# Last stage of a two-layer model: the norm's closing steps, the finish of the last block, and who forms the remainders of the running sums

## The chip, the cores and the metric

One core of one Trainium2 chip. The metric is the device time of one execution in microseconds (us). The kernel before took 3646.28 us (median of 3 runs, 3641.34 to 3650.77). All times below are us unless ns is written.

## The reference, cut to what matters

Two layers, one after the other, on x of shape (2, 2048, 512). The first is an attention layer with a feed-forward part and is not touched. The second is the last stage of the kernel, called `average` in the code:

```python
def _L1_cond_ref(inputs, vector, attention_weights, temperature, values, operator, ff1, ff1_bias, ff2, ff2_bias, ln_gamma, ln_beta):
    att = ...                                        # one gate per token and head
    v = jnp.einsum('bsi,ihk->bshk', inputs, values)
    cumv = jnp.cumsum(v, axis=1)                     # running sum over the tokens
    attn_out = att[..., None] * cumv / denom[..., None]
    op = attn_out.reshape(...) @ operator + vector[:, None, :]
    res = jax.nn.relu(jnp.concatenate([inputs, op], -1) @ ff1 + ff1_bias)
    res = res @ ff2 + ff2_bias + inputs
    mu = jnp.mean(res, axis=-1, keepdims=True)
    var = jnp.mean(jnp.square(res - mu), axis=-1, keepdims=True)
    xhat = (res - mu) * jax.lax.rsqrt(var + EPS_LN)
    return xhat * ln_gamma + ln_beta
```

## The kernel before, in words

`program` runs four stages; `average` (from L1450) is the last. It works on NA = 8 blocks of 512 tokens. Every matmul operand is held as two rounded parts, a high one (names in h: `ch`, `ah`, `sh`, `xh`) and the remainder, a low one (`cl`, `al`, `sl`, `xl`), and each product is three passes: high by high, high by the weight's low part, low by high. The running sum over tokens is taken on the input (a scan on VectorE, `running_sum`, L1760) and multiplied by the values weights afterwards.

Each engine has a program of its own, and semaphores order them. TensorE's order (the loop that follows `rows_out`) is written out by hand. For block n it is:

1. `values(n, 0)`: 12 matmuls (L1626). The first four wait for `c_hi` (the four high parts of the block's running sums, ScalarE's `sum_hi`, L1690), the last four for `c_lo` (their remainders, GpSimd's `sum_lo`, L1857).
2. `open_relu(n)`: 48 matmuls (L1609), the input's share of the hidden layer, into four PSUM accumulators.
3. `rows_out(n-1, j)` for the four tiles j of 128 tokens of the block before: 48 matmuls (L1655), the product with ff2.
4. For h = 1 to 7: `values(n, h)` and `gated(n, h-1)` (L1641), 12 matmuls each; then `gated(n, 7)`.

VectorE multiplies each `values` result by its gate (`av_full`, L1834), ScalarE rounds it (`av_gated_hi`, L1735), GpSimd forms the remainder (`av_gated_lo`, L1875); `gated(n, h)` needs both. Between these, VectorE does the norm of the block before: adds the residual rows (L1769) and takes the statistics (L1773 to L1780) at h = 0, and at h = 1 to 4 one tile each of `normed`: (row - mean) * rstd (L1789), then times gamma (L1794). GpSimd adds beta (`shifted`, L1852) and SyncE stores the tile (L1554). At h = 4 to 7 VectorE also does, for one quarter each of the next block, `zT_lo` (L1745, after ScalarE's `zT_hi`, L1680) and `running_sum` (L1760 and a small copy, L1762), and GpSimd adds the bias b2 to one tile (`zb`, L1886).

After `gated(n, 7)` ScalarE takes the hidden layer out of PSUM: `relu` (L1700) into `av_full` and a rounding copy (L1705) for each of four accumulators, from the third on only when GpSimd has formed the remainder (L1870) of the one two before, since `av_full` has two buffers. GpSimd's program has its four `sum_lo` ahead of these remainders.

The last block has nothing beside it: `relu`, the remainders, `rows_out` for four tiles, and then on VectorE two halves of two tiles each (`HALVES`), with the normalising of the first half placed after the statistics of the second.

## Time and profile before

| | |
|---|---|
| median of 3 runs (range) | 3646.28 (3641.34 to 3650.77) |
| the profiled execution: its time | 3638.28 |
| its span, first to last instruction | 3636.5 |
| mean granted TensorE clock, share of 2.4 GHz | 0.976 |
| the stage `average`, within the span | from about 3009 to 3636.5 |
| busy in the span: TensorE, VectorE, ScalarE, GpSimd | 95%, 56%, 42%, 57% |

The profile comes from one profiled execution; every time in its rows is us from the start of the span. "Busy" is the time in which an engine had an instruction under way. The matmuls are pipelined: a group of twelve takes 2.80 from the start of its first to the start of the next group, though each is listed with about 0.4. In a row of the timeline the last bracket is the idle time ahead of the instruction and what ended it.

### The profile page before, as it was taken

To read this page: it belongs to the slowest core of one execution; us is meant where nothing else is said; L and a number is where in the kernel's file an instruction comes from. 1 tells how busy PE (TensorE), PEld (TensorE's weight loads), DVE (VectorE), ACT (ScalarE), POOL (GpSimd) and SP (SyncE) were. 2 spreads that over 40 slices of the span, in tenths; PEclk is the share of its full clock that TensorE was granted. 3 is DMA by queue.
4 is the path that set the end of the run, shared out by engine and by line. 5 is a ranking of instruction groups with operands and counts; after the bars stand their busy time and mean duration, and the time that the engine had idled before them with its cause. 6 is when DMAs were issued, how large, how long until landed. Compare 5 with 4: busy or idle time off the path is not lost. (4 is left out here: it accounts for less than half of the span.)

```text
span 3636.5 us, 47173 instructions
## 1 busy us (share of the span) xinstructions
PE 3445.7 (95%) x16672; PEld 2249.6 (62%) x16672; DVE 2049.4 (56%) x3299; ACT 1513.1 (42%) x2791; POOL 2090.9 (57%) x1663
## 2 busy tenths in 40 slices
PE   7999899999999999999999969999999986999997
PEld 6777445454554545455455348888888864777776
DVE  5776677777777777777777244222222213434433
ACT  2332366666666666666666632111111112211121
POOL 3654388888988888788888712222222213544553
PEclk9999899999999999999999979999999997999999
DMA  4555676868778786967765453212222114222220
GB/s 171 183 173 197 119 146 125 157 132 152 145 129 151 135 148 125 151 140 133 152 124 111 102 150 97 70 59 76 73 70 69 57 38 145 82 73 70 74 75 37
DMA packets 176739, 419.34 MB, mean 115 GB/s; under 512 B 15382, under 2 KB 62998, under 8 KB 151670
## 3 DMA queue, kind: packets, MB, share of 16 engines
q1 hardware_dynamic: 153606, 249.59, 26.1%
q0 software_dynamic: 22896, 166.73, 23.8%
q8 instruction: 132, 2.16, 0.3%
q14 instruction: 105, 0.86, 0.1%
HBM read 162.25 MB, written 87.03 MB: 69 GB/s over the span
## 5 line engine op out<-in xcount | busy, mean ns | idle before, releaser
L845 DVE TENSOR_REDUCE part_max<-ps_att 128x1 f32<-128x512 f32 x1972 | 1226.6, 683 | 391.7 <-PE ps_att L763 390.9
L891 ACT ACTIVATE probs<-ps_att 128x512 f32<-128x512 f32 x2048 | 1062.1, 602 | 537.4 <-PE ps_att L735 456.8
L942 POOL TENSOR_TENSOR prob_sums<-prob_sums,probs 128x512 f32<-128x512 f32 x884 | 1145.8, 1558 | 56.4 <-DMA probs<-probs 56.3
L787 PE MATMUL ps_att<-probs,v_tok 128*32 128x512 f32 x4096 | 548.1, 607 | 0.0
L1433 POOL TENSOR_TENSOR ff_g_lo<-ff_g,ff_g_hi 128x512 fp32r<-128x512 f32 x128 | 165.1, 1290 | 552.4 <-DVE ff_g_hi L1394 552.4
L735 PE MATMUL ps_att<-q_stack,k_first 97*128 97x512 f32 x768 | 326.7, 425 | 10.3 <-ACT probs L891 10.0
L735 PE MATMUL ps_att<-q_stack,k_stack 97*128 97x512 f32 x768 | 321.3, 426 | 11.1 <-ACT probs L891 10.5
L1302 ACT ACTIVATE ff_g<-ps_ff 128x512 f32<-128x512 f32 x128 | 76.7, 599 | 579.7 <-PE ps_ff L1186 579.7
L763 PE MATMUL ps_att<-k_first,q_stack 96*128 96x512 f32 x756 | 302.4, 400 | 7.2 <-DMA q_stack<-qk 7.2
L763 PE MATMUL ps_att<-k_stack,q_stack 96*128 96x512 f32 x768 | 303.7, 395 | 0.0
L735 PEld LDWEIGHTS ps_att<-q_stack,k_stack 97*128 97x128 f32 x768 | 143.8, 189 | 199.2 <-ACT probs L891 146.8
L735 PEld LDWEIGHTS ps_att<-q_stack,k_first 97*128 97x128 f32 x768 | 145.9, 190 | 194.2 <-ACT probs L891 138.3
L1875 POOL TENSOR_TENSOR av_gated_lo<-av_full,av_gated_hi 128x512 fp32r<-128x512 f32 x64 | 92.5, 1445 | 282.3 <-ACT av_gated_hi L1735 282.3
L924 POOL DMA_DIRECT2D probs<-probs x159 | 151.6, 954 | 177.2 <-PE ps_att L787 160.9
L1394 DVE CAST ff_g_hi<-ff_g 128x512 fp32r<-128x512 f32 x128 | 54.8, 428 | 299.4 <-ACT ff_g L1302 299.4
L787 PEld LDWEIGHTS ps_att<-probs,v_tok 128*32 128x32 f32 x4096 | 80.8, 108 | 183.3 <-ACT probs L891 171.6
L942 POOL TENSOR_TENSOR prob_sums<-probs 128x512 f32<-128x512 f32 x128 | 164.8, 1422 | 48.7 <-DMA probs<-probs 46.1
L553 POOL TENSOR_TENSOR rotated<-rot_a,rot_b 128x512 f32<-128x512 f32 x64 | 89.8, 1403 | 153.2 <-DVE rot_b L394 149.5
L763 PEld LDWEIGHTS ps_att<-k_first,q_stack 96*128 96x128 f32 x756 | 145.2, 192 | 34.1 <-DMA q_stack<-qk 7.8
L763 PEld LDWEIGHTS ps_att<-k_stack,q_stack 96*128 96x128 f32 x768 | 145.6, 190 | 26.3
L1834 DVE TENSOR_TENSOR av_full<-ps_avg,av_gate_rows 128x512 f32<-128x512 f32 x64 | 44.3, 692 | 191.5 <-PE ps_avg L1626 84.1
L1735 ACT ACTIVATE av_gated_hi<-av_full 128x512 fp32r<-128x512 f32 x64 | 40.5, 633 | 258.7 <-DVE av_full L1834 258.7
(202 smaller groups left out, 5795.7 us busy)
## 6 DMA issues: line engine op xcount, KB each, us to landing
probs<-probs POOLq DMA_DIRECT2D x159, 1024.0 KB, 8.6
q_stack<-qk SPq DMA_DIRECT2D x144, 128.0 KB, 7.2
qk<-rot_hi SPq DMA_DIRECT2D x64, 256.0 KB, 6.6
qk<-rot_lo SPq DMA_DIRECT2D x64, 256.0 KB, 2.5
av_gate_rows<-gate SPq DMA_DIRECT2D x64, 256.0 KB
k_stack<-qk SPq DMA_DIRECT2D x24, 512.0 KB, 11.0
k_first<-qk SPq DMA_DIRECT2D x18, 512.0 KB, 10.9
x_in_sb<-in_x SPq DMA_DIRECT2D x8, 1024.0 KB, 6.7
```

The source lines that it names most:

```text
L553: nc.gpsimd.tensor_tensor(rot[:, u % 2, :], ra[:, u % 2, :], rb[:, u % 2, :], ALU.add)\
L735: nc.tensor.matmul(sT[u % 3], kS[b][0:S3 + 1, h, k * P:(k + 1) * P], q_rows(n)[0:S3 + 1, h, :], start=True, stop=True)\
L763: nc.tensor.matmul(mx[mx_uses % 3], q_rows(n)[0:S3, h, q * P:(q + 1) * P], kS[b][0:S3, h, k * TB:(k + 1) * TB], start=True, stop=True).the ...
L787: mm = nc.tensor.matmul(o_ps[rows, :], t["v"][:, steps[w]["b"], k, rows], t["p"][:, w % PR, h, :], start=(k == 0), stop=(k == LT - 1))
L845: nc.vector.tensor_reduce(t["pm"][:, r, k:k + 1], mx[mx_uses % 3], AX.X, ALU.max)\
L891: nc.scalar.activation(t["p"][:, at % PR, h, :], sT[(at * G + h) % 3], ACT.Exp)\
L924: nc.gpsimd.dma_start(t["p"][:, w % PR], t["p"][:, (w + 1) % PR], accum_op=ALU.add).then_inc(sem, 16)
L942: nc.gpsimd.tensor_tensor(x, first, t["p"][:, w % PR, h, :], ALU.add).then_inc(s["acc_done"], 1)
L1302: nc.scalar.activation(gf[:], ps[:, 4 + u % 2, :], ACT.Gelu_apprx_tanh).then_inc(s["g"], 1)
L1394: nc.vector.tensor_copy(gh[:, u % 2, :], gf[:]).then_inc(s["g_hi"], 1)
L1433: nc.gpsimd.tensor_tensor(gl[:, u % 2, :], gf[:], gh[:, u % 2, :].bitcast(F32), ALU.subtract)\
L1875: nc.gpsimd.tensor_tensor(al[:, v % 2, :], af[:, v % 2, :], ah[:, v % 2, :].bitcast(F32), ALU.subtract).then_inc(s["a_lo"], 1)
```

## The change

- The norm's closing steps become two operations with two tensors and a scalar each (scalar_tensor_tensor), both on VectorE: `centred`, (row - mean) * gamma, and `normed`, row * rstd + beta. GpSimd's `shifted` and the semaphore `ga` are gone; the store waits for `normed`.
- `zT_hi`, `zT_lo` and `running_sum` of the next block run at h = 3 to 6 instead of 4 to 7. `sum_hi` of the first quarter stands at h = 7 ahead of that h's rounding copy; the other three stay behind it.
- `sum_lo` of quarters 0 and 1 goes to VectorE, behind h = 7, for every block but the first; quarters 2 and 3 stay on GpSimd.
- Last block: ScalarE writes the rounded hidden layer straight out of PSUM (`last_relu`); VectorE recomputes it unrounded and forms the remainders (`last_relu_lo`). TensorE starts on the first accumulator that is ready, and runs the two passes on high parts of tiles 0 and 1 before their third passes (`last_rows_out`). VectorE takes the four tiles one by one through all steps.

```diff
--- before.py
+++ after.py
@@ -1491,13 +1491,12 @@
             uses += [("af", n, h) for h in range(1, HC)] if n < NA else []
         at_use = {u: i for i, u in enumerate(uses)}
         per_block = {"t": TT, "af": HC}
-        HALVES = (slice(0, 2), slice(2, TT))
         parts = ((a["ff1"], fh, fl, slice(0, 4)), (a["values"], vh, vl, slice(0, 2)), (a["values"], vh, vl, slice(2, 4)),
                  (a["wp"], wh, wl, slice(0, 4)), (a["wp"], wh, wl, slice(4, 8)), (a["ff2"], eh, el, slice(0, 4)))
         weights = [[x[:, at, :].rearrange("p k n -> p (k n)") for x in (src, hi, lo)] for src, hi, lo, at in parts]
         stage = [x.rearrange("p j f -> p (j f)") for x in (z[:, 0], z[:, 1], zTr[:, 1])]
         FF1, VAL, WP, FF2 = 0, 2, 3, 5
-        LOW_POOL = 3
+        LOW_POOL, PARTS_AT, SUMS_DVE = 3, HC - DC - 1, (0, 1)
 
         def bank(*use):
             return ring[at_use[use] % 4]
@@ -1642,19 +1641,33 @@
                                                   stop=(h == HC - 1 and i == 2))
                     mm.then_inc(s["aw"], 1)
 
-                def rows_out(n, j):
-                    pe.wait_ge(s["r_hi"], DC * (n + 1))
-                    wait_bank(pe, "t", n, j)
+                def rows_out(n, j, passes=range(3)):
+                    if 0 in passes:
+                        wait_bank(pe, "t", n, j)
                     if n == 0 and j == 0:
                         pe.wait_ge(s["w_hi"], FF2 + 1)
                         wait_low(pe, FF2)
-                    for i, (x, y) in enumerate(((sh, eh), (sh, el), (sl, eh))):
+                    for i in passes:
+                        x, y = ((sh, eh), (sh, el), (sl, eh))[i]
                         if i == 2 and j == 0:
                             pe.wait_ge(s["r_lo"], DC * (n + 1))
                         for m in range(DC):
+                            if i == 0 and j == 0:
+                                pe.wait_ge(s["r_hi"], DC * n + m + 1)
                             mm = nc.tensor.matmul(bank("t", n, j), x[:, m, j * P:(j + 1) * P], y[:, m, :],
                                                   start=(i == 0 and m == 0), stop=(i == 2 and m == DC - 1))
-                    mm.then_inc(s["ff"], 1)
+                    if 2 in passes:
+                        mm.then_inc(s["ff"], 1)
+
+                def last_rows_out(n):
+
+
+                    rows_out(n, 0, (0, 1))
+                    rows_out(n, 1, (0, 1))
+                    rows_out(n, 0, (2,))
+                    rows_out(n, 1, (2,))
+                    for j in range(2, TT):
+                        rows_out(n, j)
 
                 for n in range(NA + 1):
                     if n == 0:
@@ -1663,8 +1676,10 @@
                         values(n, 0)
                     if 0 < n < NA:
                         open_relu(n)
-                    for j in range(TT if n else 0):
+                    for j in range(TT if 0 < n < NA else 0):
                         rows_out(n - 1, j)
+                    if n == NA:
+                        last_rows_out(n - 1)
                     if n < NA:
                         for h in range(1, HC):
                             values(n, h)
@@ -1715,28 +1730,38 @@
                     sum_hi(0, f)
                 for i in range(LOW_POOL, len(weights)):
                     weight_hi(i)
+                def last_relu(n):
+                    act.wait_ge(s["aw"], (n + 1) * (HC + 1))
+                    act.wait_ge(s["ff"], TT * n)
+                    for m in range(DC):
+                        nc.scalar.activation(sh[:, m, :], acc[m], ACT.Relu, bias=bias[:, m, n // NB:n // NB + 1])\
+                            .then_inc(s["r_hi"], 1)
+
                 def root(part, js):
                     act.wait_ge(s["var"], part + 1)
                     nc.scalar.activation(sd[:, js], va[:, js], ACT.Sqrt).then_inc(s["root"], 1)
 
                 for n in range(NA + 1):
-                    for f in range(DC if 0 < n < NA else 0):
+                    for f in range(1 if 0 < n < NA else DC, DC):
                         sum_hi(n, f)
-                    if n:
+                    if 0 < n < NA:
                         relu(n - 1)
                     if n == NA:
-                        for i, js in enumerate(HALVES):
-                            root(n - 1 + i, js)
+                        last_relu(n - 1)
+                        for j in range(TT):
+                            root(n - 1 + j, slice(j, j + 1))
                     for h in range(HC if n < NA else 0):
                         v = n * HC + h
+                        if h == HC - 1 and n + 1 < NA:
+                            sum_hi(n + 1, 0)
                         act.wait_ge(s["af"], v + 1)
                         if v >= 2:
                             act.wait_ge(s["aw"], ((v - 2) // HC) * (HC + 1) + 2 + (v - 2) % HC)
                         nc.scalar.activation(ah[:, v % 2, :], af[:, v % 2, :], ACT.Copy).then_inc(s["a_hi"], 1)
                         if n and h == 0:
                             root(n - 1, slice(0, TT))
-                        if n + 1 < NA and h >= HC - DC:
-                            zT_hi(n + 1, h - (HC - DC))
+                        if n + 1 < NA and PARTS_AT <= h < PARTS_AT + DC:
+                            zT_hi(n + 1, h - PARTS_AT)
 
             @block.vector
             def _(dve):
@@ -1784,14 +1809,37 @@
                     nc.vector.reciprocal(rs[:, js], sd[:, js]).then_inc(s["rstd"], 1)
                     dve.wait_ge(s["rstd"], part + 1)
 
-                def normed(n, j):
-                    row = z[:, n % 2, j, :]
-                    nc.vector.tensor_scalar(row, row, mv[:, j, 0:1], rs[:, j:j + 1], ALU.subtract,
-                                            ALU.mult).then_inc(s["xn"], 1)
-                    dve.wait_ge(s["xn"], n * TT + j + 1)
+                def sum_lo(n, f):
+                    dve.wait_ge(s["c_hi"], n * DC + f + 1)
+                    nc.vector.tensor_tensor(cl[:, f, :], zTr[:, n % 2, f, :], ch[:, f, :].bitcast(F32), ALU.subtract)\
+                        .then_inc(s["c_lo"], 1)
+
+                def centred(n, j):
                     if n == 0 and j == 0:
                         dve.wait_ge(s["const_in"], 48)
-                    nc.vector.tensor_tensor(row, row, ga[:], ALU.mult).then_inc(s["ga"], 1)
+                    row = z[:, n % 2, j, :]
+                    nc.vector.scalar_tensor_tensor(out=row, in0=row, scalar=mv[:, j, 0:1], in1=ga[:], op0=ALU.subtract,
+                                                   op1=ALU.mult).then_inc(s["xn"], 1)
+
+                def normed(n, j):
+                    dve.wait_ge(s["xn"], n * TT + j + 1)
+                    row = z[:, n % 2, j, :]
+                    nc.vector.scalar_tensor_tensor(out=row, in0=row, scalar=rs[:, j:j + 1], in1=be[:], op0=ALU.mult,
+                                                   op1=ALU.add).then_inc(s["o"], 1)
+
+                def last_relu_lo(n):
+                    for m in range(DC):
+                        u = n * DC + m
+                        dve.wait_ge(s["r_hi"], u + 1)
+                        if m < 2:
+                            dve.wait_ge(s["a_lo"], HC * (n + 1))
+                        else:
+                            dve.wait_ge(s["r_lo"], u - 1)
+                        nc.vector.tensor_scalar(af[:, u % 2, :], acc[m], bias[:, m, n // NB:n // NB + 1], 0.0, ALU.add, ALU.max)\
+                            .then_inc(s["rf"], 1)
+                        dve.wait_ge(s["rf"], u + 1)
+                        nc.vector.tensor_tensor(sl[:, m, :], af[:, u % 2, :], sh[:, m, :].bitcast(F32), ALU.subtract)\
+                            .then_inc(s["r_lo"], 1)
 
                 dve.wait_ge(s["lg_in"], 16 * (2 * B + 2))
                 nc.vector.tensor_reduce(mx[:], am[:], AX.X, ALU.max).then_inc(s["gmax"], 1)
@@ -1814,13 +1862,13 @@
                     weight_lo(i)
                 for n in range(NA + 1):
                     if n == NA:
-                        for part, js in enumerate(HALVES):
-                            rows_in(n - 1, range(js.start, js.stop))
-                            variance(n - 1, js)
-                        for part, js in enumerate(HALVES):
-                            rstd(n - 1 + part, js)
-                            for j in range(js.start, js.stop):
-                                normed(n - 1, j)
+                        last_relu_lo(n - 1)
+                        for j in range(TT):
+                            rows_in(n - 1, (j,))
+                            variance(n - 1, slice(j, j + 1))
+                            centred(n - 1, j)
+                            rstd(n - 1 + j, slice(j, j + 1))
+                            normed(n - 1, j)
                     for h in range(HC if n < NA else 0):
                         v = n * HC + h
                         dve.wait_ge(s["cumv"], v + 1)
@@ -1840,26 +1888,26 @@
                         if n and h == 1:
                             rstd(n - 1)
                         if n and 1 <= h <= TT:
+                            centred(n - 1, h - 1)
                             normed(n - 1, h - 1)
-                        if n + 1 < NA and h >= HC - DC:
-                            zT_lo(n + 1, h - (HC - DC))
-                            running_sum(n + 1, h - (HC - DC))
+                        if n + 1 < NA and PARTS_AT <= h < PARTS_AT + DC:
+                            zT_lo(n + 1, h - PARTS_AT)
+                            running_sum(n + 1, h - PARTS_AT)
+                    for f in SUMS_DVE if n + 1 < NA else ():
+                        sum_lo(n + 1, f)
 
             @block.gpsimd
             def _(pool):
-                def shifted(n, j):
-                    pool.wait_ge(s["ga"], n * TT + j + 1)
-                    nc.gpsimd.tensor_tensor(z[:, n % 2, j, :], z[:, n % 2, j, :], be[:], ALU.add).then_inc(s["o"], 1)
-
                 def sum_lo(n, f):
                     u = n * DC + f
                     pool.wait_ge(s["c_hi"], u + 1)
                     nc.gpsimd.tensor_tensor(cl[:, f, :], zTr[:, n % 2, f, :], ch[:, f, :].bitcast(F32), ALU.subtract)\
                         .then_inc(s["c_lo"], 1)
 
-                for n in range(NA + 1):
-                    for f in range(DC if n < NA else 0):
-                        sum_lo(n, f)
+                for n in range(NA):
+                    for f in range(DC):
+                        if n == 0 or f not in SUMS_DVE:
+                            sum_lo(n, f)
                     for i in range(LOW_POOL if n == 0 else len(weights), len(weights)):
                         pool.wait_ge(s["w_hi"], i + 1)
                         nc.gpsimd.tensor_tensor(weights[i][2], stage[i % 3], weights[i][1].bitcast(F32),
@@ -1869,13 +1917,11 @@
                         pool.wait_ge(s["r_hi"], u + 1)
                         nc.gpsimd.tensor_tensor(sl[:, m, :], af[:, u % 2, :], sh[:, m, :].bitcast(F32),
                                                 ALU.subtract).then_inc(s["r_lo"], 1)
-                    for h in range(HC if n < NA else 0):
+                    for h in range(HC):
                         v = n * HC + h
                         pool.wait_ge(s["a_hi"], v + 1)
                         nc.gpsimd.tensor_tensor(al[:, v % 2, :], af[:, v % 2, :], ah[:, v % 2, :].bitcast(F32),
                                                 ALU.subtract).then_inc(s["a_lo"], 1)
-                        if n and 1 <= h <= TT:
-                            shifted(n - 1, h - 1)
                         if h >= HC - TT:
 
                             j = h - (HC - TT)
@@ -1885,8 +1931,6 @@
                                     pool.wait_ge(s["const_in"], 48)
                             nc.gpsimd.tensor_tensor(z[:, n % 2, j, :], z[:, n % 2, j, :], b2[:], ALU.add)\
                                 .then_inc(s["zb"], 1)
-                    for j in range(TT if n == NA else 0):
-                        shifted(n - 1, j)
 
 
 def program(nc, a, stop=9):
```

## Rows read from the trace of the kernel before

**Rows 1.** The page, part 1: busy time of each engine over the span.

```profile
PE 3445.7 (95%) x16672; PEld 2249.6 (62%) x16672; DVE 2049.4 (56%) x3299; ACT 1513.1 (42%) x2791; POOL 2090.9 (57%) x1663
```

**Rows 2.** Chain that ended last, blocks 5 to 6: start, duration, engine, tile, line.

```profile
3387.54 5.87 POOL av_cum_lo L1857 x4
3393.45 1.20 PE ps_avg L1626 x4
3394.65 12.50 PE ps_avg L1609 x48
3407.15 10.88 PE ps_avg L1655 x48
```

**Rows 3.** Timeline of TensorE: boundary of blocks 0 and 1, then of 5 and 6.

```profile
3109.43 1.19 PE L1626 MATMUL ps_avg<-av_cum_lo,val_hi 128*128 128x512 f32 x4 [0.31 <-POOL av_cum_lo L1857]
...
3385.90 0.50 PE L1641 MATMUL ps_avg<-av_gated_lo,wp_hi 128*128 128x512 f32 x1
...
3389.43 1.16 PE L1626 MATMUL ps_avg<-av_cum_hi,val_hi 128*128 128x512 f32 x4 [0.93 <-ACT av_cum_hi L1690]
...
3393.45 1.20 PE L1626 MATMUL ps_avg<-av_cum_lo,val_hi 128*128 128x512 f32 x4 [1.93 <-POOL av_cum_lo L1857]
```

**Rows 4.** Windows on `open_relu`: length, busy times (PE, PEld, DVE, ACT, POOL), granted clock, DMA.

```profile
3181.60:3193.30 11.70, 11.70 (x50) 9.55 (x49) 0.69 (x1) 2.47 (x4) 4.32 (x4) 0.93 0.31 100
3252.60:3263.50 10.90, 10.90 (x50) 9.01 (x49) 0.69 (x1) 3.16 (x5) 5.16 (x5) 1.00 0.31 95
3394.60:3407.10 12.50, 12.50 (x50) 10.14 (x49) 0.69 (x1) 3.16 (x5) 5.15 (x5) 0.86 0.32 93
```

**Rows 5.** Timeline of VectorE: block 5, all of h = 4, starts of h = 5 and 7.

```profile
3365.87 0.69 DVE L1834 TENSOR_TENSOR av_full<-ps_avg,av_gate_rows 128x512 f32<-128x512 f32 x1 [3.73 <-PE ps_avg L1626]
3366.48 0.54 DVE L1789 TENSOR_SCALAR av_z_sb<-av_z_sb,av_mv,av_rs 128x512 f32<-128x512 f32 x1
3367.05 0.69 DVE L1794 TENSOR_TENSOR av_z_sb<-av_z_sb,gamma_rows 128x512 f32<-128x512 f32 x1
3367.79 1.66 DVE L1745 TENSOR_TENSOR av_zT_lo<-av_zT,av_zT_hi 128x512 fp32r<-128x512 f32 x1
3369.48 2.19 DVE L1760 TENSOR_TENSOR_SCAN av_zT<-ones,av_carry_sb,av_zT 128x512 f32<-128x512 f32 x1
...
3371.82 0.69 DVE L1834 TENSOR_TENSOR av_full<-ps_avg,av_gate_rows 128x512 f32<-128x512 f32 x1
...
3383.11 0.69 DVE L1834 TENSOR_TENSOR av_full<-ps_avg,av_gate_rows 128x512 f32<-128x512 f32 x1
```

**Rows 6.** Timeline of GpSimd in the same h = 4.

```profile
3367.31 1.59 POOL L1875 TENSOR_TENSOR av_gated_lo<-av_full,av_gated_hi 128x512 fp32r<-128x512 f32 x1 [2.77 <-ACT av_gated_hi L1735]
3368.86 1.73 POOL L1852 TENSOR_TENSOR av_z_sb<-av_z_sb,beta_rows 128x512 f32<-128x512 f32 x1
```

**Rows 7.** Single lines, whole trace: duration in ns, min/median/max.

```profile
L1760 DVE TENSOR_TENSOR_SCAN av_zT<-ones,av_zT x8: 1216/2133/2203, 3029.1 to 3314.6; 128x512 f32<-128x512 f32 x8
...
L1326 DVE SCALAR_TENSOR_TENSOR w_lo<-ff_z,ln_scale_sb,w_hi x16: 735/740/1849, 2120.3 to 2207.8; 128x512 fp32r<-128x512 f32 x16
```

**Rows 8.** Chain that ended last, after the last block's `gated`.

```profile
3603.67 0.70 ACT av_full L1700
...
3609.21 13.07 PE ps_avg L1655 x48
```

**Rows 9.** Timeline of VectorE in the last block's norm.

```profile
3617.48 1.28 DVE L1773 BATCH_NORM_STATS2 av_st<-av_z_sb 128x6 f32<-128x512 f32 x2
3618.79 0.25 DVE L1778 BATCH_NORM_AGGREGATE av_mv<-av_st 128x2 f32<-128x6 f32 x2
3619.07 0.17 DVE L1780 TENSOR_SCALAR av_va<-av_mv 128x2 f32<-128x2 f32 x1
...
3624.59 0.16 DVE L1784 RECIPROCAL av_rs<-av_sd 128x2 f32<-128x2 f32 x1
```

**Rows 10.** Timeline of GpSimd: its last instruction.

```profile
3632.73 1.26 POOL L1852 TENSOR_TENSOR av_z_sb<-av_z_sb,beta_rows 128x512 f32<-128x512 f32 x1 [0.63 <-DVE av_z_sb L1794]
```

## What the change will do to the time

> **What bounds the kernel now.** First part 1 of the page: TensorE is busy 95% of the span [rows 1], so a saving has to come out of a stretch in which TensorE stands or runs slowly. The change touches only the last stage, so next the chain that ended last, within this stage: the reader sees a pattern that repeats per block. TensorE carries nearly all of it; at each boundary between two blocks the chain leaves TensorE for GpSimd, which forms four remainders of running sums in 5.87, and behind them `open_relu` takes 12.50 where the equally long `rows_out` takes 10.88 [rows 2]. Then TensorE's timeline at that boundary. Twelve matmuls take 2.80, one every 0.233 (10.88 / 48 = 0.227 in the other two products). There are three stops. (a) The third matmul of `gated(5, 7)` starts at 3385.90 instead of 3385.74: 0.16 behind GpSimd's remainder. Ten matmuls later, at 3388.23, `values(6, 0)` should start. (b) It starts at 3389.43, released by the high part of the last running sum: 1.2 lost. (c) Its eight first matmuls end their issue at about 3391.35; the third pass starts at 3393.45, released by the remainders: 2.1 lost [rows 3]. Last the granted clock: in four of six such boundaries `open_relu` takes 12.5 at a granted clock of 0.86, in one 11.7 at 0.93 (there the `values` group in front of it is stretched by another 0.8), in one 10.9 at 1.00 [rows 4]. Behind the stops the clock falls to its lower level (1.2 of 2.4 GHz) for some microseconds, which costs 12.5 - 10.9 = 1.6, five times in six.
>
> The seventh boundary, between blocks 0 and 1, is another case: TensorE is already late by gate loads there, and waits 0.31 only [rows 3].
>
> At the end of the kernel the chain runs through ScalarE (from 3603.67), TensorE (3609.21 for 13.07, 2.0 over the usual 10.88 and 0.2 drain), VectorE's norm and GpSimd's last addition, which ends at 3633.99 [rows 8, 10]. The span ends 2.5 behind that, with the store.
>
> **Part 1: the norm's steps in steady state.** Removed from VectorE: 0.54 and 0.69 per tile [rows 5]; added: two three-operand operations. The nearest row is the one at L1326, same shape: 0.74, at most 1.85 [rows 7]. From GpSimd 1.3 to 1.7 per tile go away [rows 6], which is no gain by itself, since GpSimd has spare time inside a block. At h = 1 and 2 VectorE is idle behind the norm, so the 0.2 more costs nothing; its cover is the 3.73 in front of the next gate product [rows 5].
>
> What counts is h = 3 and 4, since the scans move to h = 3 to 6. The rows at h = 4 show how VectorE and GpSimd hold each other up. `zT_lo` (the same kind of operation as the gamma product of 0.69) starts at 3367.79 and ends at 3369.45, 0.55 behind the end of GpSimd's remainder at 3368.90; that remainder took 1.59 and not 1.3, ending 1.16 behind the gamma product (3367.74). The scan ends 1.08 behind GpSimd's next operation (3370.59) [rows 5, 6], and takes 1.22 where GpSimd is idle [rows 7]. So one waits until the other's instruction is over. The Trainium skill, page "SBUF — State Buffer", section "Who interferes with whom", states this as an exclusive lock for the whole instruction, between a VectorE instruction with two SBUF inputs and a GpSimd one that reads SBUF, and that the order of issue decides who waits; this trace agrees (0.55 and 1.16 are what is left of an instruction when the other has ended). By that page the change makes more of it, since both new operations have two SBUF inputs.
>
> With that pattern h = 4 after the change: gate product 0.61, `centred` to 1.35, `normed` 1.38 to 2.12 (the gamma product ended at 1.87 before), and behind it the same sequence with `zb` in the place of `shifted`: 5.95 + 0.25 = 6.20. At h = 3 GpSimd has one remainder only, so the scan runs free: 2.12 + 1.16 + 0.55 + 0.04 + 1.22 + 0.15 = 5.2, under TensorE's 5.60 per h, and nothing carries over. So the gate product of h = 7 starts 0.25 later than now (3383.11), and stop (a) grows from 0.16 to about 0.4. Bounds: 0 later if `normed` slips in as fast as the gamma product, 0.4 if it always lands behind GpSimd's remainder.
>
> **Part 2: the boundary.** At h = 7 VectorE now has no scan, so all four running sums are done before. ScalarE rounds the first ahead of h = 7's copy, at a time when it only waits for that gate product, and the others right behind; they are there some 3 before `values(6, 0)` starts: stop (b), 1.2, goes. Remainders, on the clock of block 5: VectorE forms the first while GpSimd is idle; the second waits for the gated remainder (it ends just before 3385.90 now [rows 3], so at 3386.09 with the 0.25) and ends at 3386.64; GpSimd's `zb` ends 1.16 later at 3387.80, its two remainders, 1.28 each beside an idle VectorE (1.26 in [rows 10]), at 3390.36. TensorE: `gated(5, 7)` to 3388.48, eight matmuls to 3390.4. So the third pass starts at about 3390.45 instead of 3393.45: 3.0 saved, six times: 18.0. It is close: any lateness of VectorE goes straight into it. The boundary of blocks 0 and 1 gives 0.3. Sum 18.3. Next late is stop (a) with 0.4, and behind it the `relu` remainders, which start 3 earlier too.
>
> **Part 3: the clock.** With the idle time of a boundary down from 3.4 to about 0.4 I expect no fall of the granted clock there: 5 x 1.6 = 8.0. The bounds are 0 and 8.0; I take 8.0, because `rows_out`, which has no stop in front of it, takes the 10.88 [rows 2] that belong to a granted clock of 1.00 [rows 4], and the one boundary without a fall shows that even the longer stop is near the edge.
>
> **Part 4: the last block.** ScalarE writes the first rounded accumulator by 3603.67 + 0.70, and TensorE starts at about 3604.45 instead of 3609.21. Four outputs of 0.70 at most bring the fourth by 3606.5; twelve further matmuls end their issue at 3609.4. VectorE forms the remainders alone: per accumulator one read of PSUM (0.69, as the gate product) and one subtraction (0.69), 1.4 with the wait between: 3604.4 + 5.6 = 3610.0. So TensorE waits 0.6 for them, and tile 0 is out at 3610.0 + 4 x 0.227 + 0.2 = 3611.1, the others at 3612.0, 3614.7 and 3617.4. Then VectorE is the bound. One tile: addition 0.72, statistics 0.68, aggregate 0.17, epsilon 0.20 [rows 9], `centred` 0.66 (which hides ScalarE's root of 0.2), reciprocal 0.19, `normed` 0.6 to 0.74: 3.2 per tile with GpSimd idle. Four tiles: 3611.1 + 12.8 = 3623.9, against 3633.99 now: 10.1. For a slow clock at the start, which cost 2.0 before and of which at most 0.9 would reach tile 0 here, I take off 0.5: 9.6. Bounds 8 and 10.5.
>
> **Sum.** 18.3 + 8.0 + 9.6 = 35.9. The profiled execution took 3638.28 with a span of 3636.5, so it would take 3602.4. It lies 8 below the median of the runs; the same saving taken from 3646.28 gives 3610.4.
>
> **Rivals.** (1) *The clock falls all the same*, since a stop of 0.4 stays and the sparse matmuls of the last block remain: 8.0 come back, 3618.4. For it: it falls in five of six boundaries, with no visible difference from the sixth. Against it: `rows_out` never shows it. The Trainium skill, "TensorE: Matmul & The Clock Gate", section "What's actually happening", says that the slow level is the default and that activity releases it; by it the fall should go with the stops, as forecast. (2) *The lock lets VectorE lose more.* `normed` is issued within 0.1 of GpSimd's gated remainder, 1.38 against 1.44 behind the gate product. If it always loses at h = 4 the price is 0.15 more per boundary, 3611.3; if it and its neighbours are hit oftener, with 1 to 2 per boundary, 6 to 12: 3616 to 3622. (3) *The other side: VectorE becomes the bound of the block.* If both new operations take the 1.85 of the slowest row [rows 7] at h = 3 and 4, h = 3 takes 5.2 + 2.2 = 7.4 and h = 4 8.4, 4.6 beyond TensorE's cadence, nothing of which is caught up at h = 5 and 6 (11.29 for two, from 3371.82 to 3383.11 [rows 5]); the gate product of h = 7 is that late, TensorE stops for it at `gated(n, 7)`, and the clock's 8.0 are not gained. 18.3 + 9.6 - 6 x 4.6 = 0.3: this is the point from which it decides. If the scan at h = 3 is held up too (2.19 for 1.22), 5.6 late: about 3652, slower than before. Against it: the row of 1.85 is a maximum, the median is 0.74, and GpSimd has one operation less at h = 3. (4) *The last block's matmuls run at the lower clock throughout*, since they start sparsely: 48 x 0.45 = 22, tile 3 out at about 3627 and the end at 3633 or so: 6.5 come back, 3617.
>
> **Chances.** Forecast 0.68, rival 1 0.10, rival 2 beyond 1 per boundary 0.12, rival 3 at its break-even 0.03 and past it 0.02, rival 4 0.05. What a measurement of this kernel can tell from no change is about 0.3%, 11: the forecast and rivals 1, 2 and 4 are all faster by more. Faster 0.95, same 0.03, slower 0.02. The range: from 3602 (all bounds on the good side and 5 for the spread of the runs) to 3622 (rival 1 with such a spread, most of rival 2).
>
> **What would show it.** Right: the chain no longer leaves TensorE for the running-sum remainders; periods of a block near 67.1 (22.4 each for `values` and `gated`, 10.9 each for the two others, 0.5 of stops); windows on `open_relu` at 10.9 with a granted clock of 1.00; a wait of some 0.4 for the gated remainder at each `gated(n, 7)`; the end 19 to 21 behind ScalarE's first output of the last block, where it is 30.3 now (3633.99 - 3603.67). Wrong: a wait of over 1 at `gated(n, 7)`, three-operand rows well over 0.8 at h = 3 and 4, or a granted clock that still falls.

## The result

| | before | after |
|---|---|---|
| median of 5 runs (range) | 3650.77 (3641.34 to 3660.72) | 3614.98 (3612.37 to 3615.98) |
| time of the profiled execution | 3638.28 | 3615.76 |
| its span | 3636.5 | 3614.0 |
| start of the last stage in it | 3009.28 | 3024.66 |
| the last stage, start to end of the span | 627.2 | 589.3 |

The ratio is 0.9898, 95% interval 0.9875 to 0.9921: 35.8 less by the medians, against 35.9 forecast. The predicted time was 3610.4, the measured one 3615.0, within the range. Of the 4.6 between them 4.5 are the reference: the kernel before has a median of 3650.8 here, not the 3646.3 of the first three runs. That the two differences of medians agree to 0.1 is luck: by the interval of the ratio the saving lies between 29 and 46. The sharper measure is the last stage, which is 37.9 shorter, 2.0 more than forecast.

The two profiled spans differ by 22.5 only. The difference lies ahead of the change: the last stage's first load is issued 15.4 later in the changed kernel's execution, behind code that is the same. The stage itself is 37.9 shorter. Here is this load in the timeline of SyncE's queue: before, after, and in a second execution of the changed kernel.

```profile
3009.28 0.38 SPq L1542 DMA_DIRECT2D av_zT<-zT  x1
```

```profile
3024.66 0.38 SPq L1541 DMA_DIRECT2D av_zT<-zT  x1
```

```profile
3029.11 0.38 SPq L1541 DMA_DIRECT2D av_zT<-zT  x1
```

In the nine profiled executions of its variants below it lies between 3010.8 and 3032.5; it moves with the falls of the clock ahead of it (last section). So spans can't be compared to better than about 20. The stage repeats to 0.1 in the two executions of the changed kernel (589.34 and 589.39), though its first block can move by 1 (see "Mis-sized" below), and the periods of the blocks repeat to 0.03. The comparisons below use the stage and its parts.

**The profile after.** The chain that ended last, at the boundary of blocks 4 and 5 (start, duration, engine, tile, line), which answers to [rows 2]. (Rows 2, 3 and 5 and the prediction call the same place blocks 5 and 6; counted from 0, as in the code, it is 4 and 5.)

```profile
3385.18 0.64 ACT av_gated_hi L1760
3385.89 1.30 POOL av_gated_lo L1923
3387.23 2.60 PE ps_avg L1640 x10
3389.83 2.81 PE ps_avg L1625 x12
3392.63 10.92 PE ps_avg L1608 x48
3403.55 10.88 PE ps_avg L1657 x48
```

The remainders of the running sums are gone from it; what is left outside TensorE is the gated remainder of h = 7 (stop a). `open_relu` takes 10.92 and not 12.50. TensorE's timeline there, which answers to [rows 3] (in the bracket, idle time and what ended it):

```profile
3387.23 0.50 PE L1640 MATMUL ps_avg<-av_gated_lo,wp_hi 128*128 128x512 f32 x1 [0.28 <-POOL av_gated_lo L1923]
...
3389.67 1.09 PE L1625 MATMUL ps_avg<-av_cum_hi,val_hi 128*128 128x512 f32 x4
3390.60 1.09 PE L1625 MATMUL ps_avg<-av_cum_hi,val_lo 128*128 128x512 f32 x4
3391.53 1.11 PE L1625 MATMUL ps_avg<-av_cum_lo,val_hi 128*128 128x512 f32 x4
```

The three passes of `values(5, 0)` follow each other without a gap: stops (b) and (c) are zero. The window on the next `open_relu`, which answers to [rows 4]; its last three numbers are granted clock, DMA share and GB/s:

```profile
3392.60:3403.50 10.90, 10.90 (x50) 8.99 (x49) 0.69 (x1) 3.16 (x5) 5.21 (x5) 1.00 0.35 107
```

All seven read so. VectorE at h = 4 and 7 of block 4, which answers to [rows 5], and GpSimd beside it:

```profile
3366.93 0.69 DVE L1882 TENSOR_TENSOR av_full<-ps_avg,av_gate_rows 128x512 f32<-128x512 f32 x1 [0.26 <-PE ps_avg L1625]
3367.54 0.74 DVE L1821 SCALAR_TENSOR_TENSOR av_z_sb<-av_z_sb,av_mv,gamma_rows 128x512 f32<-128x512 f32 x1
3368.32 0.75 DVE L1827 SCALAR_TENSOR_TENSOR av_z_sb<-av_z_sb,av_rs,beta_rows 128x512 f32<-128x512 f32 x1
3368.99 1.79 DVE L1770 TENSOR_TENSOR av_zT_lo<-av_zT,av_zT_hi 128x512 fp32r<-128x512 f32 x1
3370.81 2.20 DVE L1785 TENSOR_TENSOR_SCAN av_zT<-ones,av_carry_sb,av_zT 128x512 f32<-128x512 f32 x1
...
3373.15 0.69 DVE L1882 TENSOR_TENSOR av_full<-ps_avg,av_gate_rows 128x512 f32<-128x512 f32 x1
...
3386.36 1.37 DVE L1814 TENSOR_TENSOR av_cum_lo<-av_zT,av_cum_hi 128x512 fp32r<-128x512 f32 x1 [0.62 <-ACT av_cum_hi L1705]
```

```profile
3368.37 1.86 POOL L1923 TENSOR_TENSOR av_gated_lo<-av_full,av_gated_hi 128x512 fp32r<-128x512 f32 x1 [3.74 <-ACT av_gated_hi L1760]
3370.18 1.74 POOL L1932 TENSOR_TENSOR av_z_sb<-av_z_sb,ff_bias_rows 128x512 f32<-128x512 f32 x1
...
3388.84 2.54 POOL L1904 TENSOR_TENSOR av_cum_lo<-av_zT,av_cum_hi 128x512 fp32r<-128x512 f32 x2
```

h = 4 takes 3373.15 - 3366.93 = 6.22 (6.20 forecast, 5.95 before). `normed` starts 1.39 behind the gate product, GpSimd's remainder 1.44: `normed` wins, and GpSimd's 1.86 is its usual 1.3 and a wait for VectorE. GpSimd's two remainders end at 3391.38, the third pass starts at 3391.53.

Where the 37.9 of the stage come from, by the starts of TensorE's groups in the two traces:

| part | before | after | saved | forecast |
|---|---|---|---|---|
| stage start to `open_relu(1)` | 101.2 | 99.3 | 1.9 | 0.3 |
| `open_relu(1)` to the last block's first ScalarE output | 493.2 | 466.8 | 26.4 | 26.0 |
| that output to the end of the norm | 30.3 | 20.75 | 9.6 | 9.6 |
| end of the norm to end of span | 2.5 | 2.5 | 0 | 0 |

### The profile page after: what moved, and what is told of

It is laid out like the page before. It is cut to its first block and busy times, and to the rows that moved or that the text cites. A ratio compares the mean times of both kernels' runs of the same rounds, so it can differ in the third digit from the quotient of the medians.

```text
span 3614.0 us, 47126 instructions
## 1 busy us (share of the span) xinstructions
PE 3442.8 (95%) x16672; PEld 2248.1 (62%) x16672; DVE 2076.8 (57%) x3325; ACT 1512.3 (42%) x2789; POOL 2019.2 (56%) x1613
## 5 line engine op out<-in xcount | busy, mean ns | idle before, releaser
L1186 PE MATMUL ps_ff<-ff_h_hi,w_hi 128*128 128x512 f32 x512 | 143.3, 402 | 0.7 <-ACT ff_h_hi L1314 0.7
L1201 PE MATMUL ps_ff<-w_hi,ff_g_hi 128*128 128x512 f32 x512 | 141.5, 398 | 0.0
## 6 DMA issues: line engine op xcount, KB each, us to landing
k_stack<-qk SPq DMA_DIRECT2D x24, 512.0 KB, 10.9
k_first<-qk SPq DMA_DIRECT2D x18, 512.0 KB, 10.9
```

What stands on the lines that cost most here:

```text
L1186: mm = nc.tensor.matmul(ps[:, 4 + u % 2, :], w[:, f, m * P:(m + 1) * P], h[:, f, :], start=(i == 0 and f == 0), stop=(i == 2 and f == DC - 1))
L1201: mm = nc.tensor.matmul(ps[:, j, :], g[:, u % 2, j * P:(j + 1) * P], w[:, m, :], start=(m == 0 and i == 0), stop=(m == MC - 1 and i == 2))
```

## The experiments

All start from the changed kernel. "Period" is from one `open_relu` to the next, for blocks 2 to 7 of the stage: 67.12 to 67.15 in the changed kernel, 70.2 to 71.8 before. "Finish" is from ScalarE's first output of the last block to the end of the norm. Each of e1 to e5, e7 and e9 ran once, so each rests on one trace. Their times (3610.0, 3636.3, 3616.6, 3610.5 and 3619.2 for e1 to e5, 3631.4 for e7, 3616.9 for e9) move with the start of the stage: e1 and e4 took less time than the changed kernel, with a longer stage.

**e1, the last block's finish as before, with the new norm steps.**

```diff
-        last_relu_lo(n - 1)
-        for j in range(TT):
-            rows_in(n - 1, (j,)); variance(...); centred(n - 1, j); rstd(...); normed(n - 1, j)
+        for part, js in enumerate(HALVES):
+            rows_in(n - 1, range(js.start, js.stop)); variance(n - 1, js)
+        for part, js in enumerate(HALVES):
+            rstd(n - 1 + part, js)
+            for j in range(js.start, js.stop):
+                centred(n - 1, j); normed(n - 1, j)
```

(and `relu`, its remainders on GpSimd, and the plain order on TensorE)

> The changed kernel with the last block's finish put back as before (ScalarE's two-step relu, remainders on GpSimd, four tiles through TensorE in plain order, VectorE's norm in two halves), but with the three-operand norm steps. My theory: the finish (from ScalarE's first output to the end of the last norm step) takes 20.75 in the changed kernel and 30.3 before; here TensorE ends 18.6 after the first output as before (the granted clock falls again, 2.0 of it), statistics of the second half end 2.3 later, and four pairs of three-operand steps at 1.43 follow: 26.9. So part 4 is worth 6.1 of the 9.6 by itself and 3.4 come from GpSimd being out of the norm. Rival (it is mostly GpSimd's removal): 24 or less. Blocks before the last: period 67.1, unchanged.

Measured: period 67.13, finish 3605.71 - 3579.68 = 26.0 (30.3 before, 20.75 after). VectorE's last steps (timeline of e1):

```profile
3597.15 0.69 DVE L1782 TENSOR_TENSOR av_z_sb<-ps_avg,av_z_sb 128x512 f32<-128x512 f32 x1 [2.03 <-PE ps_avg L1658]
...
3604.96 0.75 DVE L1815 SCALAR_TENSOR_TENSOR av_z_sb<-av_z_sb,av_rs,beta_rows 128x512 f32<-128x512 f32 x1
```

So 4.3 of the 9.6 are kept. Of these 1.2 come from TensorE: this variant keeps the wait per accumulator, so the first matmul starts 1.55 behind ScalarE's first output, not 5.5, and tile 3 is out 1.2 sooner than before (the granted clock was at its lower level for 3.4 there and for 6.8 before, so part of the 1.2 can be the clock). The other 3.1 lie behind tile 3 and come with GpSimd out of the norm. The new finish gives the remaining 5.3. I had 6.1 for the latter and left that early start out.

**e2, all four remainders on GpSimd.**

```diff
-        LOW_POOL, PARTS_AT, SUMS_DVE = 3, HC - DC - 1, (0, 1)
+        LOW_POOL, PARTS_AT, SUMS_DVE = 3, HC - DC - 1, ()
```

> The changed kernel with all four running-sum remainders on GpSimd again; the scans stay at h = 3 to 6. My theory: the high parts are on time (no stop b), the third pass of values(n, 0) waits for remainders that end 2 x 1.3 - 0.45 = 2.1 later, so the period is 69.2 to 69.3 instead of 67.1, 13 in six boundaries. For the clock: if it falls on any stop of 2, open_relu takes 12.5 at a granted clock of 0.86 in most boundaries and the period is 70.8; if it needs the 3.3 in two stops of before, open_relu stays at 10.9. I lean to the second at 60%.

Measured: period 69.10 to 69.14. One stop of 2.0 is added to stop (a), with no fall of the clock behind it (timeline of TensorE in e2, then the window on `open_relu`):

```profile
3407.99 1.20 PE L1625 MATMUL ps_avg<-av_cum_lo,val_hi 128*128 128x512 f32 x4 [1.73 <-POOL av_cum_lo L1904]
```

```profile
3409.10:3420.00 10.90, 10.90 (x50) 8.99 (x49) 0.69 (x1) 3.16 (x5) 5.21 (x5) 1.00 0.33 98
```

The split is worth 2.0 per block on top of the moved scans.

**e3, the scans at h = 4 to 7 again, the split kept.**

```diff
-        LOW_POOL, PARTS_AT, SUMS_DVE = 3, HC - DC - 1, (0, 1)
+        LOW_POOL, PARTS_AT, SUMS_DVE = 3, HC - DC, (0, 1)
```

> The changed kernel with the scans put back to h = 4 to 7; two remainders stay on VectorE. My theory: the fourth running sum is late again, so values(n+1, 0) starts 1.1 late (stop b), and VectorE's two remainders, now behind the last scan, make the third pass wait another 0.4 to 1.0: period 68.6 to 69.2. Rival (moving the scans is worth nothing, the split of the remainders is what counts): period 67.1 to 67.5. Clock as in the run beside it: two short stops, 1.5 to 2 in all; I expect no fall.

Measured: period 69.02 to 69.04, and `open_relu` stays at 10.9. Two shorter stops, 1.1 and 0.7, are added to stop (a) (timeline of TensorE in e3):

```profile
3385.26 1.16 PE L1625 MATMUL ps_avg<-av_cum_hi,val_hi 128*128 128x512 f32 x4 [0.93 <-ACT av_cum_hi L1705]
...
3387.83 1.20 PE L1625 MATMUL ps_avg<-av_cum_lo,val_hi 128*128 128x512 f32 x4 [0.47 <-DVE av_cum_lo L1814]
```

Moving the scans is worth 1.9 on top of the split.

**e4, the norm's steps as before, in all blocks but the last.**

```diff
-                            centred(n - 1, h - 1)
-                            normed(n - 1, h - 1)
+                            old_normed(n - 1, h - 1)   # tensor_scalar, then times gamma
...
+                        if n and 1 <= h <= TT:
+                            shifted(n - 1, h - 1)      # GpSimd adds beta
```

> The changed kernel with the norm's steps of all blocks but the last as before (two-operand steps on VectorE, beta on GpSimd). My theory: part 1 is worth next to nothing in steady state. GpSimd's addition holds up the scan at h = 3 too (2.2 for 1.28), so h = 3 takes 5.95 and h = 4 5.95: the gate product of h = 7 starts 0.8 late against 0.7 in the changed kernel; period 67.1 to 67.3. Rival (the three-operand steps are what made room for the scans at h = 3): period 68 or more. The opposite (they cost by the exclusive port): 66.8 or less.

Measured: period 67.22, 0.1 more than in the changed kernel. VectorE in e4, the end of h = 4:

```profile
3365.11 2.19 DVE L1785 TENSOR_TENSOR_SCAN av_zT<-ones,av_carry_sb,av_zT 128x512 f32<-128x512 f32 x1
...
3367.45 0.69 DVE L1891 TENSOR_TENSOR av_full<-ps_avg,av_gate_rows 128x512 f32<-128x512 f32 x1
```

As expected, h = 3 and h = 4 take 5.95 and 5.94. So the three-operand steps are worth 0.1 per block in steady state: their longer time on VectorE (1.49 for 1.23 per tile) and the work taken from GpSimd nearly cancel.

**e7, scans late and all remainders on GpSimd.**

```diff
-        LOW_POOL, PARTS_AT, SUMS_DVE = 3, HC - DC - 1, (0, 1)
+        LOW_POOL, PARTS_AT, SUMS_DVE = 3, HC - DC, ()
```

> The scans back at h = 4 to 7 and all four remainders on GpSimd: of the change only the norm's steps, the early rounding of the first running sum and the last block's finish are left. Taking back only one of the two parts gave periods of 69.03 and 69.12 with no fall of the clock. My theory: both stops of before return (about 1.1 and 2.1), so 70.2 to 70.4 by idle time alone; and with both the granted clock falls again behind them in most boundaries: open_relu 12.5 at 0.86 and a period of 71.8 there. Rival (the fall of the clock in the kernel before had another cause than these stops, in the norm's steps or in GpSimd's work): period 70.2 throughout and open_relu 10.9.

Measured: periods 70.45, 70.49, 72.40, 72.36, 71.37, 70.47. Both stops are back, and with them falls of the granted clock at four of six boundaries (windows on `open_relu` of blocks 3, 4 and 2, then TensorE ahead of block 5):

```profile
3253.50:3264.40 10.90, 10.90 (x42) 8.87 (x41) 0.69 (x1) 3.16 (x5) 5.25 (x5) 0.85 0.31 93
3325.90:3338.40 12.50, 12.50 (x51) 10.21 (x50) 0.69 (x1) 3.02 (x5) 4.91 (x4) 0.90 0.32 94
...
3183.00:3193.90 10.90, 10.90 (x49) 9.01 (x48) 0.69 (x1) 3.16 (x5) 5.31 (x5) 1.00 0.30 90
```

```profile
3392.56 1.17 PE L1625 MATMUL ps_avg<-av_cum_hi,val_hi 128*128 128x512 f32 x4 [0.93 <-ACT av_cum_hi L1705]
3396.58 1.92 PE L1625 MATMUL ps_avg<-av_cum_lo,val_hi 128*128 128x512 f32 x4 [1.91 <-POOL av_cum_lo L1904]
```

This, e2 and e3 tie the falls of the clock to the two stops. With 3.3 of idle time in two stops some boundaries keep the upper level and some lose it; with one stop of 2.0 (e2), or 1.1 and 0.7 (e3), none of the twelve boundaries from block 1 on lost it (the periods are all within 0.04). In all of these stop (a) lies ahead. Each part of the change by itself already keeps the clock, so the parts don't add: either brings the period from 71.3 (mean of before) to 69.1, the second from there to 67.1.

**e9, TensorE's four last tiles in plain order.**

```diff
-                        last_rows_out(n - 1)
+                        for j in range(TT):
+                            rows_out(n - 1, j)
```

> The changed kernel with TensorE's four tiles of the last block in plain order again: tile 0 with all three passes, then tile 1 and so on. VectorE and ScalarE as in the changed kernel. Tile 0 can't end before the remainders, at the same time as now; tile 1 then ends 12 matmuls later, 2.7, while VectorE needs 3.25 for tile 0. Theory: VectorE's norm per tile is the bound, so the order is worth nothing and the finish, from ScalarE's first output to the end of the norm, stays at 20.75 (to 20.9). Rival (TensorE's order carries part of the gain): 22.5, since TensorE stands for 2.7 longer ahead of the remainders and ends later. A third reading: with only 4 to 8 matmuls issued before the longer wait for the remainders the granted clock falls and the finish takes 1 to 2 more.

Measured: finish 3612.41 - 3590.59 = 21.8, 1.1 more than after, and it was the third reading. TensorE in e9, and a window:

```profile
3597.00 1.29 PE L1657 MATMUL ps_avg<-ff_hi,av_relu_lo 128*128 128x512 f32 x4 [2.52 <-DVE av_relu_lo L1842]
3598.09 1.91 PE L1657 MATMUL ps_avg<-ff_hi,av_relu_hi 128*128 128x512 f32 x4
```

```profile
3598.00:3600.00 2.00, 2.00 (x6) 0.50 0.00 0
```

At full clock the sixteen matmuls up to the end of tile 1 take 3.8, so it would have been out at 3600.8, ahead of VectorE (free at about 3601.6 by the cadence of 3.25); at half clock it is out at 3602.54, and VectorE waits. So the 1.1 are the clock's, and by this count the order of the passes would be worth nothing at full clock. That the plain order, with its longer wait, brings the fall about is not shown: this is one execution, and the clock fell in the last block with the new order too, in e3 and e7, two of the nine executions that have it. There it fell behind the first four matmuls, tile 0 came 0.6 later, and the finish took 21.4. In e3, a window, and VectorE's first tile:

```profile
3593.50:3597.00 3.50, 3.50 (x9) 2.72 (x10) 3.40 (x6) 0.00 (x0) 0.00 (x0) 0.51 0.00 0
```

```profile
3599.21 0.69 DVE L1794 TENSOR_TENSOR av_z_sb<-ps_avg,av_z_sb 128x512 f32<-128x512 f32 x1 [1.92 <-PE ps_avg L1657]
```

Where both orders meet a fall, they differ by 0.45.

**e5, the changed kernel with GpSimd's bias addition moved to h = 0 to 3.**

```diff
-                        if h >= HC - TT:
-                            j = h - (HC - TT)
+                        zb_at = 0 if n else HC - TT
+                        if zb_at <= h < zb_at + TT:
+                            j = h - zb_at
```

> The changed kernel with GpSimd's bias addition (zb) moved from h = 4 to 7 to h = 0 to 3, in all blocks but the first. If VectorE's lateness of 0.7 at h = 7 comes from waiting for GpSimd's instructions over the shared access (my theory), the scans at h = 5 and 6 drop from 2.2 to 1.28, VectorE catches up before h = 7, the stop at the third matmul of gated(n, 7) goes from 0.5 to under 0.1 and the period from 67.13 to 66.6 to 66.7: 3 over six boundaries. Rival (the scan with a carry is slow by itself, 2.2 whatever GpSimd does, as all 24 were in the kernel before): period 67.1, unchanged.

Measured: period 66.60 in all six, and no stop is left at these boundaries; stage 584.9, which is 4.4 less than in the changed kernel: 3.2 from the six periods, and 1.2 from block 0, where the code is the same (see "Mis-sized"). VectorE in e5, scans at h = 3, 4 and 6, and the gate product of h = 7:

```profile
3370.06 2.20 DVE L1785 TENSOR_TENSOR_SCAN av_zT<-ones,av_carry_sb,av_zT 128x512 f32<-128x512 f32 x1
...
3376.27 1.28 DVE L1785 TENSOR_TENSOR_SCAN av_zT<-ones,av_carry_sb,av_zT 128x512 f32<-128x512 f32 x1
...
3386.30 1.28 DVE L1785 TENSOR_TENSOR_SCAN av_zT<-ones,av_carry_sb,av_zT 128x512 f32<-128x512 f32 x1
...
3388.59 0.69 DVE L1882 TENSOR_TENSOR av_full<-ps_avg,av_gate_rows 128x512 f32<-128x512 f32 x1 [0.81 <-PE ps_avg L1625]
```

The scan takes 2.20 only where GpSimd's addition runs beside it (h = 3), and 1.28 elsewhere: the extra 0.9 was waiting. The changed kernel shows the mirror image: 1.28 at h = 3, where GpSimd has no addition, and 2.20 at h = 4 to 6. VectorE now waits for TensorE at h = 7.

**e6, e5 with block 0's loads in another order.** After and before, the gate products of h = 3 and 4 of block 0 waited for their gate rows, behind constants, z(0) and zT(1) in the queue.

```diff
                 for i in range(1, 5):
                     load_weight(i)
+                    if i == 3:                          # the three constant rows, moved up
+                        for dst, src in ((b2, "ff2_bias"), (ga, "gamma"), (be, "beta")): ...
...
-                        if h == 0 and n + 1 < NA:
+                        if h == (0 if n else 1) and n + 1 < NA:
                             load_zT(n + 1)
+                        if n == 0 and h == 1:
+                            load_z(0)
```

> As e5_bias_early, and in block 0 the three constant rows are loaded ahead of the fifth weight load, and z(0) and zT(1) behind the gate rows of h = 4, since the gate products of h = 3 and 4 waited 9.8 and 2.4 for their gate rows there, which stood in the queue behind 2 MB of other loads. Theory: open_relu(0) to open_relu(1) takes 89.0 in the changed kernel and 80 to 84 here; all in all 8 to 12 less than the changed kernel beside it. Rival (the gate rows' own pace of 5.1 each, two source rows spread over 128 partitions, sets block 0): 87 or more.

Measured: median 3606.18 (5 runs), 0.9876 of the kernel before (0.9856 to 0.9897); stage 583.35, 6.0 less than the changed kernel, not 8 to 12. Block 0 takes 85.99 from `open_relu(0)` to `open_relu(1)`, not 80 to 84 (89.0 in the changed kernel, 87.85 in e5). The new order of the loads is worth about 1.9 of it: e5 differs from e6 in the loads alone. The gate rows of h = 3 were on time, but the input of the scans was not (timeline of ScalarE in e6):

```profile
3086.70 0.63 ACT L1697 ACTIVATE av_zT_hi<-av_zT 128x512 fp32r<-128x512 f32 x1 [6.66 <-DMA av_zT<-zT]
```

**The changed kernel again, beside e6.**

> The changed kernel again, as it stands, for a comparison beside the kernel before and the run above on one chip: 0.9895 of the kernel before by my sum (35.9 less), 0.9938 if only the difference of the two profiled executions counts (22.5 less, since the last stage began 15.4 later in the changed kernel's). I hold that the start of the last stage moves by this much from one execution to the next whatever the kernel: in the profiles of the changed kernel and its four variants it lies at 3024.7, 3014.6, 3032.5, 3013.0 and 3018.2, and the code ahead of it is the same. So 0.9895, and a stage of 589.3 here again.

Measured: median 3616.16 (6 runs), ratio 0.9901 (0.9880 to 0.9922); stage 589.39, with its start at 3029.11.

**e8, zT(1) ahead of the gate rows of h = 4 again, z(0) behind those of h = 5.**

```diff
-                        if n == 0 and h == 1:
+                        if n == 0 and h == 2:
                             load_z(0)
```

(`load_zT(1)` at h = 0)

> As e6_loads_moved, but zT(1) is loaded ahead of the gate rows of h = 4 (as in the changed kernel) and only z(0) behind those of h = 5. There the gate rows of h = 3 were on time, and what was late next was zT(1): ScalarE waited 6.66 for it, VectorE 7.99, and the gate product of h = 4 with it. Theory: with zT(1) some 5 earlier, open_relu(0) to open_relu(1) falls from 86.0 to 81 to 83. Rival: the 1 MB of zT(1) now delays the gate rows of h = 4 by as much, and it stays at 85 to 87.

Measured: median 3602.61 (4 runs), 0.9862 of the kernel before (0.9834 to 0.9891); stage 581.8. Block 0 takes 84.6, between the two readings: the gate rows of h = 4 and 6 are late by 2.8 and 2.6 again. It has the lowest median of all; from the changed kernel it is 7.6 away in the stage, where parts can be compared, and 12 to 14 by the medians, which move with the start of the stage.

## Why the prediction was right

The forecast was right in its mechanism, term by term, with one term mis-sized.

**Stops (b) and (c)**, 3.0 per boundary: the third pass was to start 3.0 earlier, and the period was to be near 67.1. It is 67.13. The stop (a) that stays costs 0.53, which is 67.13 less the period of 66.60 that e5 has without any stop; I had about 0.4. e2 and e3 show that both parts are needed (expected ahead of these runs 69.2 to 69.3, measured 69.12; expected 68.6 to 69.2, measured 69.03).

**h = 3 and 4 on VectorE**: 5.2 and 6.2 worked out, 6.22 measured at h = 4; at h = 3 VectorE waited 0.26 for TensorE, so nothing carried over. The pattern of waiting behind each other's instruction, on which this rested, holds in e5.

**The clock**, 8.0: `open_relu` reads 10.9 at a granted clock of 1.00 in all seven blocks. Together with the stops 26.4 were saved where 26.0 were forecast. e7 supports the cause: with both stops back the falls are back. The 8.0 is the price of the falls in one execution of the kernel before, which has five; e7 has four, with the same two stops.

**The last block**: TensorE started at 3591.57, 0.83 behind ScalarE's first output (0.78 forecast), stood 0.7 for the remainders (0.6), tile 0 was out 7.65 behind the first output (7.4), and VectorE then took 3.25 per tile (3.2). The rows that answer to [rows 8, 9], ScalarE, TensorE, and VectorE's first tile:

```profile
3590.74 2.42 ACT L1737 ACTIVATE av_relu_hi<-ps_avg,bias_all 128x512 fp32r<-128x512 f32 x4 [4.24 <-PE ps_avg L1640]
```

```profile
3591.57 2.14 PE L1657 MATMUL ps_avg<-ff_hi,av_relu_hi 128*128 128x512 f32 x4 [0.87 <-ACT av_relu_hi L1737]
...
3597.16 2.12 PE L1657 MATMUL ps_avg<-ff_hi,av_relu_lo 128*128 128x512 f32 x8 [0.68 <-DVE av_relu_lo L1841]
```

```profile
3598.39 0.69 DVE L1794 TENSOR_TENSOR av_z_sb<-ps_avg,av_z_sb 128x512 f32<-128x512 f32 x1 [1.29 <-PE ps_avg L1657]
...
3601.66 0.68 DVE L1794 TENSOR_TENSOR av_z_sb<-ps_avg,av_z_sb 128x512 f32<-128x512 f32 x1
...
3610.74 0.75 DVE L1827 SCALAR_TENSOR_TENSOR av_z_sb<-av_z_sb,av_rs,beta_rows 128x512 f32<-128x512 f32 x1
```

The 0.5 that I took off for a slow clock at the start was not needed in this execution; it was used up by 0.2 more up to tile 0, and 0.3 more in the four tiles (13.1 for 12.8). That the 9.6 came out exactly is in part luck: in e3 and e7 the clock did fall at the start, which cost 0.6 (finish 21.4).

**Mis-sized:** the boundary of blocks 0 and 1 gave 1.9, not 0.3. I read only the 0.31 of TensorE's wait there, and left out that TensorE ran at its lower level just ahead of it. Three windows: on the fall before, on the fall after, and on the last 14 ahead of `open_relu(1)` in e1:

```profile
3101.20:3108.00 6.80, 6.18 (x16) 4.80 (x16) 3.48 (x3) 3.41 (x7) 6.80 (x5) 0.50 0.51 162
```

```profile
3117.10:3120.50 3.40, 3.28 (x8) 2.60 (x9) 0.61 (x1) 0.27 (x1) 3.40 (x4) 0.50 0.69 220
```

```profile
3099.00:3113.00 14.00, 11.69 (x49) 8.60 (x48) 7.22 (x9) 6.51 (x11) 9.66 (x7) 1.00 0.38 115
```

The half clock lasts 6.8 before, 3.4 after, and is absent in e1 and e5, whose code in block 0 is that of the changed kernel. From the start of the stage to `open_relu(1)` they take 101.2, 99.3, 98.3 and 98.1. So the same code moves by 1 there, with the clock. The slow clock probably also hid the stops. In e7, where the order of the work at this boundary is that of before and the clock stays up, they show in full, 1.1 and 2.1, and the stretch takes 101.8. TensorE there, at the third pass:

```profile
3111.55 1.19 PE L1625 MATMUL ps_avg<-av_cum_lo,val_hi 128*128 128x512 f32 x4 [1.91 <-POOL av_cum_lo L1904]
```

How much of the 1.9 is the change's and how much chance was not tested. Part 1, on whose two operations I spent the most care, is worth 0.1 per block (e4). I had put it at a cost of 0.25 at h = 7 against the old steps at h = 4 alone; beside scans at h = 3 and 4 the old steps, with GpSimd's addition, are later still.

The rivals: rival 1 did not happen. Rival 4 did not happen in the changed kernel's own two executions; in e3, e7 and e9 the clock did fall in the last block, for 3.4 and not throughout, and it cost 0.6, 0.6 and 1.1, not 6.5. Rival 2's race was won by 0.05 at h = 2 to 4 and lost at h = 1 in every block, where it costs nothing, since VectorE waits for TensorE behind it (timeline of VectorE after, h = 1 and 2 of block 4):

```profile
3352.62 1.68 DVE L1827 SCALAR_TENSOR_TENSOR av_z_sb<-av_z_sb,av_rs,beta_rows 128x512 f32<-128x512 f32 x1
3355.73 0.69 DVE L1882 TENSOR_TENSOR av_full<-ps_avg,av_gate_rows 128x512 f32<-128x512 f32 x1 [1.43 <-PE ps_avg L1625]
```

Rival 3 is not seen: no three-operand step took more than 0.75 at h = 3 or 4, though 1.68 lay one place further on.

## What to carry to other kernels

Before crediting an idle engine's removed work, follow who waits for whom at the one point where the bounding engine stops; here the moved scans and the split remainders are worth 2 each per block once the other is there, and the operations that were fused are worth 0.1. Where VectorE and GpSimd both read two tensors from SBUF, lay their instructions out so that they don't meet: moving an addition of 1.3 to where VectorE had nothing urgent took away the last stop. Compare stages, not spans, when an earlier stage moves by as much as a good part of what the change is worth.

## What the runs showed of the hardware

- The granted clock fell behind two stops of 1.1 and 2.1 in most boundaries but not in all (five of six before, four of six in e7), with no difference between them in the rows, and not behind 2.0 in one stop or 1.8 in two. In the last block it fell behind a wait of 2.52 (e9), and in two of nine executions of the new finish behind the first four matmuls, without such a wait (e3, e7). What decides stays open.
- A scan of 128x512 with a carry takes 1.28 without GpSimd's addition beside it and 2.2 with it; all 24 rows of it before read 2.2, and the stage's only fast scans, 1.22 without a carry, were two of block 0's. A duration that never varies in a trace can still be waiting, here for 0.9 of 2.2.
- The start of the last stage moves by up to 23 between executions (3009.3 to 3032.5) with the same code ahead of it. It goes with the clock: by the traces' record of the granted clock, TensorE was at its lower level ahead of that start for 102.6 in the kernel before (start 3009.3), 129.4 and 139.5 in the changed kernel's two executions (3024.7, 3029.1) and 140.2 in e5 (3032.3), and the other executions lie close to the same line (112 at 3010.8 to 3014.6). Half of the 26.8 between before and after is 13.4, of the 15.4 by which the starts differ. Whether the falls cause the delay, or waits ahead of them cause both, was not tested. The mean over the whole execution (0.975 to 0.978) hides it.
